# Splitting a table into three bf16 parts on ScalarE and TensorE in place of VectorE, in an embedding-bag kernel

## The chip, the cores and the metric

The kernel runs on one core of one Trainium2 chip. The metric is the device time of a whole execution in microseconds (us). The kernel before takes 1639.28 us (median of 3 runs, 1639.16 to 1640.66).

## The reference

There are 32 tables of 12,500 rows of 64 fp32 numbers, 512 bags for each table, and 20 row numbers and a length for each bag. The output is, for each bag and table, the sum of the rows that the first `length` numbers name.

```python
flat = tables.reshape(F_ * V_, E_)                    # F=32, V=12500, E=64
emb = flat[ids + offs]                                # ids: (B=512, F=32, L=20)
mask = (jnp.arange(L_) < lengths[..., None]).astype(emb.dtype)
pooled = jnp.einsum('bfle,bfl->bfe', emb, mask)
return jnp.nan_to_num(pooled.reshape(Bq, F_ * E_))
```

## The kernel before

The tables are divided between two methods that run side by side.

**Counted tables (M = 18).** A table is loaded whole, 128 partitions by J = 98 rows of E = 64, in seven chunks (`CHUNKS`) of 14 rows, 896 fp32 numbers in a partition. The bags are taken in two halves, h = 0 and 1. VectorE builds one-hot matrices from the row numbers (`onehots`, L625 and L627; `single`, L611 and L613), TensorE multiplies a pair of them (`count`, L444) into a bank pair in PSUM, and ScalarE copies these counts to SBUF as small numbers (`save_counts`, L422). Such a step is called a slot here: two one-hot matmuls, one copy on ScalarE, and eight or ten matmuls of the half before it. Those (`multiply`, L454) multiply the counts with the table, which stands in three bf16 parts so that fp32 is kept. A half has 21 slots in seven stages of three, with a short single eviction ahead; a table has 14 stages, 42 slots and 44 evictions, and 18 tables make 792 evictions. The counts of half h are multiplied while the counts of the next half are made.

The three parts are the upper 16 bits of each fp32 number, the rest after them, and what is left after the upper 16 bits of that rest. VectorE makes them with two subtractions for each chunk, `cut_rest` (L641) and `cut_low` (L649), at the stages that `CUTS` gives (3 to 12), some chunks in two pieces. VectorE works `AHEAD` = 2 stages ahead of TensorE, since there are two sets of one-hots. The counts go through `SETS` = 3 sets of bank pairs: TensorE's eviction n waits until eviction n - 3 has been saved.

**Gathered tables (14).** GpSimd (POOL) gathers rows by indirect DMA, up to 20 for each of 56 tiles of 128 bags (L379), into 8 buffers. VectorE adds a tile's rows (`add_rows`, L689) at fixed stages (`ADDS`, seven tiles for two counted tables); after each fourth tile GpSimd stores the results (`put`, L389). A buffer is refilled with zeros and row numbers by SyncE after its tile was added, and GpSimd takes the buffers in order. At the start GpSimd also writes 56 tiles of sorted records to DRAM (L365).

SyncE issues the loads of the tables: `reload` waits for TensorE to be done with the chunk of the table before. All waits are on semaphores, and each engine works in its own program order. TensorE's tables 1 to 17 are a loop (L495).

```python
free = n - (SETS - 2 if h == 0 and c == 0 and q < 1 else SETS - 1)
if not known(free, 1):
    pe.wait_ge(counts_saved, free)
```

Of the kernel before, what the change touches and what calls it, by code (L numbers as in the profile page):

```python
# [23 lines left out]
P = 128  # L24
# [3 lines left out]
SETS = 3  # L28
PARTS = 3
CHUNKS = 7  # L30
PER_CHUNK = 6
PAIRS = PER_CHUNK // 2
AHEAD = 2
# [7 lines left out]
CUTS = {3: (0, 0, 1), 4: (1, 0, 1), 5: (2, 0, 2), 6: (2, 1, 2), 7: (3, 0, 2), 8: (3, 1, 2), 9: (4, 0, 1),  # L41
        10: (5, 0, 2), 11: (5, 1, 2), 12: (6, 0, 1)}
# [33 lines left out]
def build_embedding_bag(nc, ids, lengths, tables, lookup_ids, lookup_lengths, lookup_place, ramps, triangle,  # L76
# [25 lines left out]
    assert STAGES % AHEAD == 0 and P_COLUMNS % 2 == 0 and L < 32 and LAST_BAGS == 4 and 2 * EVICTIONS % SETS == 2  # L102
# [17 lines left out]
    with ExitStack() as ctx:  # L120
# [21 lines left out]
        lane = sb("lane", [P, 1], I32)  # L142
        p_of = sb("p_of", [P, HALVES, P_COLUMNS], F16)
# [64 lines left out]
        rest_done = sem("rest_done")  # L208
        parts_ready = sem("parts_ready")
# [32 lines left out]
        def eviction_at(stage, q):  # L242

            return eviction(stage // STAGES, stage // CHUNKS % 2, stage % CHUNKS, q)

# [161 lines left out]
        def _(act):  # L407
# [15 lines left out]

            for f in range(M):
                for h in range(2):
                    save_counts(f, h, 0, -1)
                    for c in range(CHUNKS):
                        for q in range(PAIRS):
                            save_counts(f, h, c, q)

        @block.tensor
        def _(pe):
# [28 lines left out]

            def phase(f, h, with_counts=True, with_products=True):
# [29 lines left out]
            rank_lengths()  # L492
            phase(0, 0, with_products=False)
# [7 lines left out]
        def _(dve):  # L501
# [86 lines left out]

            def prepare(c):
# [40 lines left out]
            def upper_halves(t):  # L630
                return table[:, t, :].bitcast(BF16).rearrange("p (n x) -> p n x", x=2)[:, :, 1]

            cuts = [0]

            def cut_rest(f, c, part, parts):

                sl = slice(c * CE + part * CE // parts, c * CE + (part + 1) * CE // parts)
                if part == 0:

                    dve.wait_ge(table_in[c], f * 16 + 16)  # L640
# [4 lines left out]
            def cut_low(f, c, part, parts):  # L645
                sl = slice(c * CE + part * CE // parts, c * CE + (part + 1) * CE // parts)
# [142 lines left out]
```

## Time and profile before

| what | value |
|---|---|
| median of 3 runs | 1639.28 us |
| profiled execution: its own time, its span | 1622.87 us, 1621.1 us |
| mean granted TensorE clock | 0.792 |
| VectorE (DVE) busy | 1065.0 us, 66% |
| TensorE matmul (PE) busy | 1003.0 us, 62% |
| GpSimd (POOL) busy | 760.1 us, 47% |
| ScalarE (ACT) busy | 509.2 us, 31% |

The busy time of an engine is a sum over the whole span. PE's matmuls overlap, so that its busy time isn't a measure of its peak. The granted clock is 1.00 at 2.4 GHz and 0.50 at 1.2 GHz. "Releaser" is what ended the idle time of an engine; "remote" or "unknown queue" stands where the profile found no record that fits, and "issue" where the engine waited for nothing that the profile shows.

### The profile page before, as it was taken

What the parts mean: (1) busy time and instruction counts of PE and PEld (TensorE: products, weight loads), DVE (VectorE), ACT (ScalarE), POOL (GpSimd) and SP (SyncE); (2) the same over time, 40 slices, a digit from 0 to 9 for tenths busy, and PEclk for the clock granted to TensorE, in tenths of its full rate; (3) what the DMA queues carried; (4) which work ended last, traced back from release to release, by engine and by line L of the source; (5) the groups of instructions that cost most, each with busy time, mean ns of one, the idle gap of its engine ahead of it and who ended that gap; (6) DMA issues with size and microseconds to landing.
All of it is one profiled execution on the core that took longest, in us unless ns stands there. A gap on an engine that the chain in (4) does not pass through costs nothing.

```text
span 1621.1 us, 25785 instructions
## 1 busy us (share of the span) xinstructions
PE 1003.0 (62%) x8607; PEld 801.0 (49%) x8607; DVE 1065.0 (66%) x3021; ACT 509.2 (31%) x793; POOL 760.1 (47%) x706
## 2 busy tenths in 40 slices
PE   2757107692754816757588582881847538487886
PEld 0536006571643715636377360760735437276776
DVE  9938006793673916947599481891857629489894
ACT  2423004350422403324244140430423214143441
POOL 4845770537064172253666527166073442556110
PEclk9979558896786957968789685895877759689899
DMA  4312112132312213132334141231314113233120
GB/s 142 137 51 56 24 25 81 53 120 61 99 55 60 91 42 103 46 92 69 82 103 129 38 120 41 85 88 37 114 43 123 52 41 98 52 111 110 31 83 11
DMA packets 69225, 121.48 MB, mean 75 GB/s; under 512 B 33985, under 2 KB 35750, under 8 KB 69152
## 3 DMA queue, kind: packets, MB, share of 16 engines
q1 hardware_dynamic: 45936, 99.21, 19.0%
q0 software_dynamic: 22016, 20.93, 7.2%
q10 hardware_dynamic: 1200, 0.67, 0.2%
q14 instruction: 65, 0.53, 0.1%
q8 instruction: 8, 0.13, 0.0%
HBM read 79.67 MB, written 4.80 MB: 52 GB/s over the span
## 4 chain that ended last, share of the span: by engine, by line
DVE 44%; another core or an unknown queue 29%; PE 14%; issue 7%; DMA 2%; ACT 2%; SPq 1%; DVEq 0%; POOL 0%; POOLq 0%
DVE onehot_j L627 16%; PE sums L454 9%; DVE onehot_p L625 6%; DVE table L641 6%; DVE table L649 6%; DVE gathered L689 5%; PE pairs L444 4%; DMA table<-tables 2%; ACT counts L422 2%; DVE is_nan L659 1%; SPq L305 1%; DVE pooled L669 1%; DVE pooled L662 0%; DVEq L687 0%
## 5 line engine op out<-in xcount | busy, mean ns | idle before, releaser
L454 PE MATMUL sums<-table,counts 128*128 128x192 bf16 x7056 | 835.5, 262 | 209.3 <-issue 202.1
L422 ACT ACTIVATE counts<-pairs 128x588 int16<-128x588 f32 (+1 forms) x792 | 507.9, 653 | 1082.1 <-remote 547.1
L454 PEld LDWEIGHTS sums<-table,counts 128*128 128x128 fp8e3 x7056 | 667.0, 102 | 312.8 <-issue 258.3
L379 POOL DMA_INDIRECT rows<-tables,row_now x576 | 618.5, 1074 | 414.6 <-issue 414.6
L444 PE MATMUL pairs<-onehot_j,onehot_p 128*128 128x294 bf16 x1548 | 383.8, 315 | 390.2 <-ACT counts L422 164.4
L625 DVE TENSOR_TENSOR onehot_p<-ramp,p_of 128x256 bf16<-128x256 f16 x756 | 213.7, 283 | 435.1 <-remote 385.0
L627 DVE TENSOR_SCALAR onehot_j<-ramp,j_of,worth 128x296 bf16<-128x296 f16 x1512 | 493.6, 358 | 0.0
L444 PEld LDWEIGHTS pairs<-onehot_j,onehot_p 128*128 128x128 bf16 x1548 | 151.4, 101 | 488.5 <-issue 264.5
L389 POOL DMA_INDIRECT out_gathered<-gathered,place_now x56 | 70.2, 1254 | 394.0 <-DVE gathered L662 381.2
L641 DVE TENSOR_TENSOR table<-table 128x448 f32<-128x448 f32 (+1 forms) x180 | 144.4, 802 | 27.7 <-DMA table<-tables 27.0
L649 DVE TENSOR_TENSOR table<-table 128x448 f32<-128x448 f32 (+1 forms) x180 | 144.7, 804 | 0.0
L689 DVE TENSOR_REDUCE gathered<-rows 128x64 f32<-128x1280 f32 x56 | 131.2, 2343 | 0.0
L365 POOL DMA_INDIRECT sorted_records<-records,rank x56 | 69.3, 1238 | 33.7 <-DVE records L517 16.9
L669 DVE TENSOR_REDUCE pooled<-sums 128x128 f32<-128x384 f32 x36 | 19.7, 546 | 80.2 <-remote 67.4
L613 DVE TENSOR_SCALAR onehot_j<-ramp,j_of,worth 128x296 bf16<-128x296 f16 x36 | 13.1, 363 | 0.0
L611 DVE TENSOR_SCALAR onehot_p<-ramp,p_of 128x128 bf16<-128x128 f16 x36 | 11.0, 305 | 0.0
L662 DVE COPY_PREDICATED pooled<-is_nan,zeros 128x256 f32<-128x256 uint8 x18 | 8.1, 450 | 0.6
L659 DVE TENSOR_TENSOR is_nan<-pooled 128x256 uint8<-128x256 f32 x18 | 7.7, 427 | 0.6
L692 DVE COPY place_now<-row_now 128x1 int32<-128x1 int32 x56 | 8.1, 144 | 0.0
L662 DVE COPY_PREDICATED gathered<-is_nan,zeros 128x256 f32<-128x256 uint8 x14 | 6.2, 446 | 0.5
L659 DVE TENSOR_TENSOR is_nan<-gathered 128x256 uint8<-128x256 f32 x14 | 6.0, 426 | 0.5
L488 PE MATMUL sums<-counts 128*128 128x21 f16 x1 | 0.2, 177 | 8.2 <-DVE counts L536 8.2
(53 smaller groups left out, 49.0 us busy)
## 6 DMA issues: line engine op xcount, KB each, us to landing
table<-tables SPq DMA_DIRECT2D x126, 448.0 KB
rows<-zeros SPq DMA_DIRECT2D x56, 640.0 KB
rows<-tables,row_now POOLq DMA_INDIRECT x576
out_counted<-pooled SPq DMA_DIRECT2D x108, 21.0 KB
sorted_records<-records,rank POOLq DMA_INDIRECT x56
row_now<-sorted_records SPq DMA_DIRECT2D x56, 10.5 KB
out_gathered<-gathered,place_now POOLq DMA_INDIRECT x56
rows<-lookup_ids SPq DMA_DIRECT2D x1, 731.0 KB, 7.8
```

The lines of the kernel that those rows point to most:

```text
L365: nc.gpsimd.indirect_dma_start(out=sorted_records, out_offset=bass.IndirectOffsetOnAxis(ap=rank[:, t:t + 1], axis=0), in_=records[:, t, :] ...
L379: nc.gpsimd.indirect_dma_start(out=rows[:, k, l * E:(l + 1) * E], out_offset=None, in_=table_rows, in_offset=bass.IndirectOffsetOnAxis(ap= ...
L389: nc.gpsimd.indirect_dma_start(out=out_gathered, out_offset=bass.IndirectOffsetOnAxis(ap=place_now[:, k:k + 1], axis=0), in_=gathered[:, k ...
L422: nc.scalar.activation(dst, src, ACT.Copy).then_inc(counts_saved, 1)
L444: last = nc.tensor.matmul(pair(h, c, q)[:, x, 0:WIDE], onehot_p[:, s, k, :, side], onehot_j[:, s, i + 1, 0:WIDE], start=True, stop=True)
L454: last = nc.tensor.matmul(sums[h][:, k * PARTS * E:(k + 1) * PARTS * E], counts[h][:, j, :, k], parts[:, :, j, :, 1], start=(j == 0 and k ...
L625: nc.vector.tensor_tensor(onehot_p[:, s, 1 + i // 2, :, :], ramp_twice, p_of[:, 2 * f + h, g:g + 2].unsqueeze(1).to_broadcast([P, P, 2]), ...
L627: nc.vector.tensor_scalar(onehot_j[:, s, i + 1, :], ramp[:, 2 * P:], j_of[:, n:n + 1], worth[:, 0:1], ALU.is_equal, ALU.mult).then_inc(one ...
L641: nc.vector.tensor_tensor(table[:, 1, sl], table[:, 0, sl], upper_halves(0)[:, sl], ALU.subtract).then_inc(rest_done, 1)
L649: cut = nc.vector.tensor_tensor(table[:, 2, sl], table[:, 1, sl], upper_halves(1)[:, sl], ALU.subtract)
L669: nc.vector.tensor_reduce(out=pooled[:, 2 * h * E:2 * (h + 1) * E].rearrange("p (k e) -> p k e", e=E), in_=sums[h][:, 0:2 * PARTS * E].rea ...
L689: nc.vector.tensor_reduce(out=gathered[:, k * E:(k + 1) * E], in_=rows[:, k, :].rearrange("p (l e) -> p e l", e=E), axis=AX_X, op=ALU.add)
```

## The change

Six of the seven chunks of each table are parted by ScalarE and TensorE; VectorE keeps the seventh. ScalarE copies a chunk of fp32 numbers into a new bank pair in PSUM, `rest` (`copy_chunk`). TensorE subtracts the upper 16 bits there, with a matmul against a negative identity matrix that accumulates (`take_away`, two matmuls of 448 columns). ScalarE writes the upper 16 bits of the rest to the second part of the table (`save_middle`), TensorE takes that away, and ScalarE writes what is left to the third part (`save_low`). The chunk begun at slot u is copied at u, has its middle saved at u + 1 and its low part at u + 2; chunks begin at slots 9, 13, 17, 21, 25 and 29. On each engine these steps stand behind the slot's own work. VectorE parts chunk 6, whole, at stage 12. The new bank pair comes from the counts: `SETS` falls from 3 to 2. VectorE makes the negative identity once (`negate_eye`), and TensorE opens `rest` once (`begin_rest`).

```diff
-SETS = 3
+SETS = 2
-CUTS = {3: (0, 0, 1), 4: (1, 0, 1), 5: (2, 0, 2), 6: (2, 1, 2), 7: (3, 0, 2), 8: (3, 1, 2), 9: (4, 0, 1),
-        10: (5, 0, 2), 11: (5, 1, 2), 12: (6, 0, 1)}
+PARTED_AT = {0: 9, 1: 13, 2: 17, 3: 21, 4: 25, 5: 29}
+PARTED_BY_VECTOR = {12: 6}
...
+        minus_eye = sb("minus_eye", [P, P], BF16)
+        rest = psum("rest", [P, 2, 512], F32)
...
+            def copy_chunk(f, c):
+                if f == 0 and c == min(PARTED_AT):
+                    act.wait_ge(rest_begun, 1)
+                elif parted(f, c) > 1:
+                    act.wait_ge(low_saved, parted(f, c) - 1)
+                act.wait_ge(table_in[c], f * 16 + 16)
+                nc.scalar.activation(rest[:, :, 0:CE // 2], both_halves(0, c), ACT.Copy).then_inc(chunk_copied, 1)
+            def save_middle(f, c):
+                act.wait_ge(rest_ready, parted(f, c))
+                nc.scalar.activation(upper_of_both(1, c), rest[:, :, 0:CE // 2], ACT.Copy).then_inc(middle_ready, 1)
+            def save_low(f, c):
+                act.wait_ge(low_ready, parted(f, c))
+                nc.scalar.activation(upper_of_both(2, c), rest[:, :, 0:CE // 2], ACT.Copy).then_inc(low_saved, 1)
...
                             save_counts(f, h, c, q)
+                            u = slot(h, c, q)
+                            if u - 2 in begun_in:
+                                save_low(f, begun_in[u - 2])
+                            if u - 1 in begun_in:
+                                save_middle(f, begun_in[u - 1])
+                            if u in begun_in:
+                                copy_chunk(f, begun_in[u])
...
+            def take_away(part, c, done):
+                for x, half in enumerate(halves_of(c)):
+                    last = nc.tensor.matmul(rest[:, x, 0:CE // 2], minus_eye[:], upper_halves(part)[:, half],
+                                            start=False, stop=True, skip_group_check=True)
+                last.then_inc(done, 1)
+            def part_table(f, u):
+                if u - 2 in begun_in:
+                    pe.wait_ge(middle_ready, parted(f, begun_in[u - 2]))
+                    take_away(1, begun_in[u - 2], low_ready)
+                if u - 1 in begun_in:
+                    pe.wait_ge(chunk_copied, parted(f, begun_in[u - 1]))
+                    take_away(0, begun_in[u - 1], rest_ready)
...
-                                pe.wait_ge(parts_ready, f * CHUNKS + (c + 1))
+                                if c in PARTED_AT:
+                                    pe.wait_ge(low_saved, parted(f, c))
+                                else:
+                                    pe.wait_ge(parts_ready, f * (CHUNKS - PARTED) + by_vector.index(c) + 1)
                             multiply(1 - h, c * JC + q * JC // PAIRS, c * JC + (q + 1) * JC // PAIRS)
+                        if with_counts:
+                            part_table(f, slot(h, c, q))
...
-                    if stage in CUTS and i == 1:
-                        cut_rest(f, *CUTS[stage])
-                    if stage in CUTS and i == 4:
-                        cut_low(f, *CUTS[stage])
+                    if stage in PARTED_BY_VECTOR and i == 1:
+                        cut_rest(f, PARTED_BY_VECTOR[stage])
+                    if stage in PARTED_BY_VECTOR and i == 4:
+                        cut_low(f, PARTED_BY_VECTOR[stage])
```

## Rows read from the trace of the kernel before

**Rows 1.** The chain that ended last, by line, whole span.

```profile
by line: another core or an unknown queue 29.3%; DVE onehot_j L627 15.7%; PE sums L454 9.5%; issue 7.1%; DVE onehot_p L625 6.1%; DVE table L641 6.0%; DVE table L649 5.5%; DVE gathered L689 5.5%; PE pairs L444 4.2%; DMA table<-tables 2.1%; A
```

**Rows 2.** The waits: us in total, times, longest.

```profile
ACT counts L422 <- remote: 547.1, 66, 32.4
...
DVE onehot_p L625 <- remote: 385.0, 52, 32.1
```

**Rows 3.** Busy time of each engine in 27 stretches in which GpSimd gathers.

```profile
core 0: us, PE busy (x) PEld busy (x) DVE busy (x) ACT busy (x) POOL busy (x), PEclk, DMA share, GB/s
134.00:245.00 111.00, 28.75 (x182) 16.57 (x179) 24.31 (x75) 9.77 (x15) 85.72 (x83) 0.60 0.14 25
...
562.00:617.00 55.00, 12.19 (x90) 9.88 (x89) 13.41 (x40) 3.98 (x6) 42.58 (x41) 0.59 0.20 44
...
817.00:847.00 30.00, 24.46 (x250) 21.42 (x247) 29.70 (x84) 14.01 (x22) 24.21 (x20) 0.97 0.32 90
...
1598.00:1603.00 5.00, 5.00 (x61) 5.00 (x59) 0.00 (x0) 0.00 (x0) 3.79 (x4) 1.00 0.06 20
sum 876.00, PE 426.83 PEld 314.29 DVE 450.51 ACT 166.82 POOL 684.21; mean PE 15.81 PEld 11.64 DVE 16.69 ACT 6.18 POOL 25.34
```

**Rows 4.** The same for the 26 stretches between them.

```profile
245.00:291.00 46.00, 34.80 (x330) 30.80 (x331) 33.26 (x97) 20.61 (x32) 0.00 (x0) 0.83 0.28 85
...
1555.00:1598.00 43.00, 37.72 (x365) 31.73 (x363) 42.81 (x114) 18.84 (x29) 0.00 (x0) 0.96 0.13 36
sum 593.00, PE 493.69 PEld 425.62 DVE 506.22 ACT 294.87 POOL 4.47; mean PE 18.99 PEld 16.37 DVE 19.47 ACT 11.34 POOL 0.17
```

**Rows 5.** TensorE's timeline, first in a gathering stretch, then in one without.

```profile
192.29 0.32 PE L454 MATMUL sums<-table,counts 128*128 128x192 bf16 x1 [2.49 <-issue]
195.09 0.32 PE L454 MATMUL sums<-table,counts 128*128 128x192 bf16 x1 [2.47 <-issue]
...
264.00 0.41 PE L444 MATMUL pairs<-onehot_j,onehot_p 128*128 128x294 bf16 x2
264.24 1.02 PE L454 MATMUL sums<-table,counts 128*128 128x192 bf16 x10
...
267.14 0.41 PE L444 MATMUL pairs<-onehot_j,onehot_p 128*128 128x294 bf16 x2
```

**Rows 6.** Groups by line and shape: busy us, mean ns, idle before.

```profile
L422 ACT ACTIVATE counts<-pairs 128x588 int16<-128x588 f32 x756 | 496.4, 667 | 975.2 <-remote 475.9 <-PE pairs L444 444.8 <-issue 53.5
L627 DVE TENSOR_SCALAR onehot_j<-ramp,j_of,worth 128x296 bf16<-128x296 f16 x1512 | 493.6, 358 | 0.0
L625 DVE TENSOR_TENSOR onehot_p<-ramp,p_of 128x256 bf16<-128x256 f16 x756 | 213.7, 283 | 435.1 <-remote 385.0 <-issue 25.6 <-PE pairs L444 24.0
L689 DVE TENSOR_REDUCE gathered<-rows 128x64 f32<-128x1280 f32 x56 | 131.2, 2343 | 0.0
L649 DVE TENSOR_TENSOR table<-table 128x896 f32<-128x896 f32 x72 | 78.1, 1085 | 0.0
L641 DVE TENSOR_TENSOR table<-table 128x896 f32<-128x896 f32 x72 | 77.9, 1082 | 27.7 <-DMA table<-tables 27.0 <-issue 0.7
L649 DVE TENSOR_TENSOR table<-table 128x448 f32<-128x448 f32 x108 | 66.6, 617 | 0.0
L641 DVE TENSOR_TENSOR table<-table 128x448 f32<-128x448 f32 x108 | 66.6, 616 | 0.0
L422 ACT ACTIVATE counts<-pairs 128x196 int16<-128x196 f32 x36 | 12.3, 341 | 106.9 <-remote 71.2 <-PE pairs L444 35.2 <-issue 0.3
L379 POOL DMA_INDIRECT rows<-tables,row_now x576 | 618.5, 1074 | 414.6 <-issue 414.6
```

**Rows 7.** GpSimd's gathers and VectorE's work beside them, timeline.

```profile
353.29 2.34 POOL L379 DMA_INDIRECT rows<-tables,row_now  x1 [0.30 <-issue]
...
353.46 1.08 DVE L641 TENSOR_TENSOR table<-table 128x896 f32<-128x896 f32 x1
...
192.83 1.00 POOL L379 DMA_INDIRECT rows<-tables,row_now  x1 [0.30 <-issue]
```

More of the change, by code:

```diff
@@ L244, in eviction_at, with slot, parted, halves_of @@
             return eviction(stage // STAGES, stage // CHUNKS % 2, stage % CHUNKS, q)
+        def slot(h, c, q):
+            return (h * CHUNKS + c) * PAIRS + q
+        by_vector = sorted(PARTED_BY_VECTOR.values())
+        begun_in = {u: c for c, u in PARTED_AT.items()}
+        PARTED = len(PARTED_AT)
+        def parted(f, c):
+            return f * PARTED + sorted(PARTED_AT).index(c) + 1
+        def halves_of(c):
+            return [slice(c * CE + x * CE // 2, c * CE + (x + 1) * CE // 2) for x in range(2)]
+        def both_halves(part, c):
+            return table[:, part, c * CE:(c + 1) * CE].rearrange("p (x n) -> p x n", x=2)
+        def upper_halves(part):
+            return table[:, part, :].bitcast(BF16).rearrange("p (n x) -> p n x", x=2)[:, :, 1]
+        def upper_of_both(part, c):
+            return upper_halves(part)[:, c * CE:(c + 1) * CE].rearrange("p (x n) -> p x n", x=2)
         def lookup_group(c, i):
@@ L460, in multiply, with begin_rest @@
                     last.then_inc(table_used, 1)
+            def begin_rest():
+                pe.wait_ge(eye_ready, 1)
+                pe.wait_ge(ramps_in, 32)
+                for x in range(2):
+                    last = nc.tensor.matmul(rest[:, x, :], minus_eye[:], ramp[:, 0:512], start=True, stop=True)
+                last.then_inc(rest_begun, 1)
+            def take_away(part, c, done):
[10 more added lines that the diff above has]
+                    take_away(0, begun_in[u - 1], rest_ready)
             def phase(f, h, with_counts=True, with_products=True):
@@ L492, in _ @@
             rank_lengths()
+            begin_rest()
             phase(0, 0, with_products=False)
@@ L628, in onehots, with cut_rest @@
                                         ALU.is_equal, ALU.mult).then_inc(onehots_ready, 1)
-            def upper_halves(t):
-                return table[:, t, :].bitcast(BF16).rearrange("p (n x) -> p n x", x=2)[:, :, 1]
             cuts = [0]
[L635 to L640, printed above, removed]
+            def cut_rest(f, c):
+                sl = slice(c * CE, (c + 1) * CE)
+                dve.wait_ge(table_in[c], f * 16 + 16)
                 nc.vector.tensor_tensor(table[:, 1, sl], table[:, 0, sl], upper_halves(0)[:, sl],
@@ L643, in cut_rest, with cut_low @@
                 cuts[0] += 1
-            def cut_low(f, c, part, parts):
-                sl = slice(c * CE + part * CE // parts, c * CE + (part + 1) * CE // parts)
+            def cut_low(f, c):
+                sl = slice(c * CE, (c + 1) * CE)
                 dve.wait_ge(rest_done, cuts[0])
-                cut = nc.vector.tensor_tensor(table[:, 2, sl], table[:, 1, sl], upper_halves(1)[:, sl], ALU.subtract)
-                if part == parts - 1:
-                    cut.then_inc(parts_ready, 1)
+                nc.vector.tensor_tensor(table[:, 2, sl], table[:, 1, sl], upper_halves(1)[:, sl],
+                                        ALU.subtract).then_inc(parts_ready, 1)
             cleaned = [0]
```

15 lines of the change are left out of this document (13 added, 2 removed).

## Prediction

> **What bounds the kernel now.** The chain that ended last is read first. Its largest part has no name: 29.3% stands under an unknown queue, and VectorE's cuts are only 6.0% and 5.5% [rows 1]. The waits say where that part lies: VectorE's L625 sat 385.0 us and ScalarE's L422 547.1 us until something for which the profile has no record [rows 2]. Both wait for TensorE's pair matmuls, so I cut the span by what GpSimd does.
>
> In 27 stretches, 876 us in all, GpSimd gathers; in the 26 between them, 593 us, it doesn't [rows 3, 4]. (134 us lie ahead and 18 behind.) ScalarE's count of instructions is the progress: one for each of the 792 evictions. By their starts 253 fall into the gathering stretches, 467 between them, and 72 ahead. So an eviction takes 876/253 = 3.46 us beside gathers and 593/467 = 1.27 us without. The stretch 562 to 617 is the extreme, 6 evictions in 55 us; 817 to 847 is the mild one, 22 in 30 [rows 3]. TensorE's own rows show the same: in the slow part one matmul of 192 columns each 2.8 us, with "issue" ahead of it, where otherwise ten take 0.86 us [rows 5]. What exactly holds TensorE beside the gathers I can't read; that it comes with them, I can. GpSimd's work is fixed, so these 876 us stay nearly whatever the others do. The kernel isn't bound by VectorE over its span, though VectorE's 66% is the highest: that is a mean over two regimes.
>
> Without gathers three slots of TensorE take 3.14 us (264.00 to 267.14) [rows 5]: 44 evictions make 44 x 1.053 = 46.3 us a table (the single one is shorter, which I leave out). VectorE's slot is 283 + 2 x 358 = 1.00 us by durations; by starts, less, since they overlap. VectorE's cuts are 78.1 + 77.9 + 66.6 + 66.6 = 289.2 us, 16.1 a table [rows 6]. VectorE and TensorE are thus near to each other, with VectorE somewhat longer in stages with cuts.
>
> **The change, part by part.**
>
> *VectorE's cuts.* Six of seven chunks go: 6/7 x 289.2 = 248 us of busy time. What of it is on the path? Between gathers the mean granted clock, weighted over the rows, is 0.858: 28% of 593, or 168 us, at half rate (1.2 GHz) [rows 4]. There TensorE needs 2.11 us an eviction and does 80. The other 425 us hold 387, 1.10 each, against TensorE's own 1.053. So VectorE can cost at most 0.045 x 387 = 17 us there. In the first half of table 0 nothing is multiplied and VectorE sets the pace: three chunks' cuts stand there (stages 3 to 6), 6 x 1.08 us by durations; I take 6 us off.
>
> *TensorE's new matmuls.* Four of 448 columns for each of six chunks, 24 a table. The pair matmuls of 294 columns follow each other such that two take 0.24 us at full clock (264.00 to 264.24) [rows 5], 0.122 each, so 448 columns take 0.187 by their columns: 4.5 us a table, 0.102 us an eviction. The 467 evictions between gathers then cost: 168 us at half rate do 168/2.31 = 73, and 394 at 1.155 take 455. That is 623 us, 30 more than 593, with VectorE's 17 us already given back. The bounds are +13 (half-rate time shrinks to half) and +48 (the 0.045 stays as hand-over time).
>
> *ScalarE.* 18 operations of 896 elements a table. From 667 ns at 588 elements and 341 at 196 [rows 6] the slope is 0.832 ns and the start 178 ns: 923 ns, 16.6 us a table, 299 in all, beside 509. In the four slots of a chunk ScalarE has 4 x 0.667 + 3 x 0.923 = 5.44 us, TensorE 4 x 1.053 + 0.75 = 4.96. Durations overlap, so I take this at 0; if they did not, 108 x 0.48 = 52 us come on top. Each save waits for TensorE behind its slot, with the next save of counts behind it on ScalarE; TensorE needs that one only two slots later. This cover is gone where a hand-over takes over one slot.
>
> *Two bank sets.* TensorE may be one slot ahead of ScalarE's saves, not two. Without gathers nothing is lost by it; beside them, where ScalarE saw a count late by several us, it is.
>
> *GpSimd.* A gather has 1074 ns in the mean and 1.00 us when alone; the one that met the cut L641 took 2.34 [rows 7]. If all were 1.00, 576 x 0.074 = 43 us would go. Most of the causes go (L625 stays): I take -25, bounds 0 and -43. The Trainium skill (SBUF — State Buffer, Who interferes with whom) says that a VectorE instruction with two SBUF inputs contends with a GpSimd instruction that reads SBUF; these rows agree.
>
> *Progress beside gathers.* In seven of the 27 stretches VectorE was at least 97% busy (529, 645, 817, 1239, 1351, 1447 and 1547): 57 evictions in 87 us. The other twenty hold 196 in 789 us, 4.0 us each. After the change VectorE is never the slowest: 1.00 us a slot against TensorE's 1.155 and ScalarE's load. I take the 87 us to go as the others: 22 evictions, 35 fewer. Each is made up between gathers at 623/467 = 1.33 us: +47 us. Bounds: all at the pace of 562 to 617 (9.2 us each) leaves 95 of 253, +210; from below, the half of today's slowing gone, 876/(3.46/2) = 506, -337. The near rows are the other twenty, so I stay by +47. The reader should doubt this term most: that an idle VectorE goes with a slow TensorE is seen, which causes which isn't.
>
> *Table loads.* VectorE's 27.0 us of waits for them [rows 6] go; they fell behind slow stretches, where TensorE had work. The copy of chunk 0 is at slot 9, after its load is in. 0 us.
>
> **The sum**, on the profiled span: 1621 + 30 - 6 - 25 + 47 = 1667 us. The median is 18 us above this span (1639.28 against 1621.1, in this one execution), so 1685 us.
>
> **The rivals.**
>
> *The stretches with gathers keep their progress.* For it: their length is GpSimd's, and TensorE is slow in them also when VectorE is full (1239 to 1250). Without the +47: 1620, or 1638 in the median, no change by what this kernel's measurement can tell (0.2%, 3 us), with 20 us on both sides.
>
> *Faster: the cuts are on the path after all.* The chain counts L641 and L649 with 11.5% of the span [rows 1]; 6/7 of it is 160 us, so 1461, or 1479 in the median. It decides if VectorE's lead, not TensorE, is what the slow stretches eat: VectorE works on in their first us and would later be the one that is behind. Against it: the sum above allows 17 us between gathers. The Trainium skill (the same page and section) says that TensorE never waits on anyone's port; by it the slow stretches would be no contention and only VectorE's 248 us would count, 1391 us in the median. The matmul each 2.8 us speaks against it.
>
> *Faster: fewer, longer matmuls load TensorE's path less beside gathers.* 14 matmuls in 1.43 us of such a slot against 12 in 1.05. If a third of 253 evictions more got through, 84 x 1.33 = 112 us go from 1620: 1508, 1526; for half of that 1564 and 1582. Nothing in the profile shows the onset well enough to refuse it.
>
> *Slower by hand-overs.* Beside gathers, a chunk crosses from TensorE to ScalarE and back twice. 253/792 of 108 chunks are 34; if each crossing costs TensorE an eviction's 3.46 us once, 34 x 2 x 3.46 = 235 us are lost there, and a third of it not covered is 78 us: 1745 us, or 1763. With ScalarE's 52 us 1815. It decides when a hand-over exceeds one slot.
>
> **How the numbers follow.** Forecast 0.42 (1650 to 1725); hand-overs 0.14 (1725 to 1815); unchanged stretches 0.18 (1615 to 1650; a third each faster, same, slower); more getting through 0.15 (1520 to 1615); cuts on the path 0.11 (1390 to 1520). Faster: 0.06 + 0.15 + 0.11 = 0.32, and 0.03 from the low edge of the forecast's bounds, 0.35. Same 0.06. Slower the rest, 0.59. The forecast's own range is 1650 to 1725. The range reaches down to 1550 and up to 1765: it leaves out 0.15 below and some 0.05 above.
>
> **What would show it.** VectorE's busy time near 817 us and ScalarE's near 808; TensorE with 432 matmuls more; a slot between gathers of 1.15 us a row at full clock; gathers at a mean of 1.03; and, decisive, ScalarE's instructions that save counts in the stretches with gathers: some 218 where there were 253. The forecast is wrong if these rise, or if the slots between gathers take less than 1.1 us, or if the stretches with gathers themselves become shorter than some 850 us.

## The result, and the profile after

The kernel after takes 1820.01 us (median of 4 runs, 1817.8 to 1823.82), the kernel before 1639.22 beside it: a ratio of 1.113, 95% interval 1.106 to 1.120. The forecast was 1685 (1550 to 1765). It is slower, as was thought likeliest, but by four times as much as forecast. Where the executions of a kernel scatter by more than 1.5%, the ratios are of its faster executions alone, and so can differ a little from the ratio of two medians.

One thing has to be said at once, though it was found last: the comparisons fell on several chips. In five of seven (the first, and chips 10, 14, 0 and 8) the kernel before has a median of 1613 to 1639 us; in the other two, on chips 6 and 9, it takes 1095. The kernel after was run on one of these two, chip 9, and takes 1026 there, a ratio of 0.937. What follows explains the first, and then the second.

The page of the kernel after, busy time of each engine, TensorE's clock by fortieths, and the chain by engine:

```profile
PE 1051.3 (58%) x9041; PEld 852.6 (47%) x9041; DVE 870.6 (48%) x2698; ACT 809.6 (45%) x1117; POOL 700.3 (39%) x706
...
PEclk9778559787777958779677786767967769678899
...
another core or an unknown queue 35%; PE 35%; ACT 13%; DVE 10%; issue 6%; POOL 0%; DVEq 0%; POOLq 0%
```

No engine is over 58% busy, and a large part of the chain still has no name (29.3% before [rows 1], 35% now). Its waits, which answer to [rows 2]:

```profile
DVE onehot_p L715 <- remote: 588.9, 74, 32.8
ACT counts L455 <- remote: 506.1, 63, 33.0
POOL out_gathered L422 <- DVE gathered L746: 427.5, 14, 58.1
...
PE pairs L500 <- ACT counts L455: 247.6, 61, 26.4
...
PE rest L528 <- ACT table L467: 170.5, 90, 25.5
```

VectorE's wait without a record has grown by 204 us; that is more than the whole loss. The busy time by stretches answers to [rows 3] and [rows 4]: first those in which GpSimd gathers, then those between.

```profile
core 0: us, PE busy (x) PEld busy (x) DVE busy (x) ACT busy (x) POOL busy (x), PEclk, DMA share, GB/s
156.00:262.00 106.00, 15.30 (x95) 10.24 (x92) 6.51 (x22) 8.64 (x11) 81.32 (x82) 0.54 0.13 26
...
sum 815.00, PE 278.09 PEld 215.55 DVE 195.94 ACT 152.49 POOL 626.78; mean PE 7.95 PEld 6.16 DVE 5.60 ACT 4.36 POOL 17.91
```

```profile
267.00:324.00 57.00, 46.71 (x440) 39.77 (x440) 38.20 (x127) 39.30 (x55) 0.40 (x2) 0.88 0.23 69
...
sum 824.00, PE 681.54 PEld 570.09 DVE 581.52 ACT 584.00 POOL 9.99; mean PE 20.05 PEld 16.77 DVE 17.10 ACT 17.18 POOL 0.29
```

Beside gathers TensorE is busy 278 of 815 us where it was 427 of 876 [rows 3], and VectorE, 451 of 876 before, is now busy 196. The stretches with gathers are shorter, but less gets done in them. The evictions are counted as the prediction did, by the starts of ScalarE's saves of counts. The stretches are taken here by the exact starts and ends of the gathers, so that before has 252 in 873 us where the text ahead has 253 in 876; a stretch ends where GpSimd pauses for over 1.5 us.

| | ahead | beside gathers | between | behind | end |
|---|---|---|---|---|---|
| before | 134 us | 873 us, 252 (3.46 each) | 596 us, 468 (1.27) | 18 | 1621 |
| after | 156 us | 819 us, 148 (5.53) | 820 us, 574 (1.43) | 21 | 1816 |

The 195 us are thus: 106 more evictions between gathers, 106 x 1.27 = +135; the stretches with gathers, -54; the pace between gathers, (1.43 - 1.27) x 574 = +89; +22 ahead and +3 behind. (Each kernel is measured here by one profiled execution, as above.)

The groups by line and shape, which answer to [rows 6]:

```profile
L412 POOL DMA_INDIRECT rows<-tables,row_now x576 | 578.1, 1004 | 619.8 <-issue 619.5 <-DMA row_now<-sorted_records 0.3
L455 ACT ACTIVATE counts<-pairs 128x588 int16<-128x588 f32 x756 | 492.3, 664 | 694.3 <-remote 488.0 <-PE pairs L500 180.1 <-issue 24.9
...
L471 ACT ACTIVATE table<-rest 128x896 bf16<-128x896 f32 x108 | 127.8, 1183 | 122.8 <-remote 102.8 <-PE rest L528 14.0 <-issue 0.5
L467 ACT ACTIVATE table<-rest 128x896 bf16<-128x896 f32 x108 | 127.1, 1177 | 122.0 <-remote 90.0 <-PE rest L528 15.2 <-issue 10.3
L463 ACT ACTIVATE rest<-table 128x896 f32<-128x896 f32 x108 | 100.4, 929 | 0.0
```

ScalarE's copy into PSUM takes 929 ns, as the slope in the prediction said (923), but its two saves to the table take 1183 and 1177. And a gather takes 1.00 us in the mean. TensorE's timeline in a stretch without gathers, at full clock, shows what a chunk costs (611.93 to 617.48 are four slots):

```profile
611.93 0.41 PE L500 MATMUL pairs<-onehot_j,onehot_p 128*128 128x294 bf16 x2
...
612.13 1.18 ACT L467 ACTIVATE table<-rest 128x896 bf16<-128x896 f32 x1
...
613.37 0.57 PE L528 MATMUL rest<-table,minus_eye 128*128 128x448 bf16 x2 [0.17 <-ACT table L467]
...
613.77 0.41 PE L500 MATMUL pairs<-onehot_j,onehot_p 128*128 128x294 bf16 x2
...
613.97 1.19 ACT L471 ACTIVATE table<-rest 128x896 bf16<-128x896 f32 x1
...
616.08 0.95 ACT L463 ACTIVATE rest<-table 128x896 f32<-128x896 f32 x1
...
617.48 0.41 PE L500 MATMUL pairs<-onehot_j,onehot_p 128*128 128x294 bf16 x2
```

Four slots with a chunk take 5.55 us, where the prediction had 4.96 for TensorE alone. The two new matmuls take 0.40 us (613.37 to 613.77), 0.80 for both hand-overs; the other 0.5 us are TensorE's waits for ScalarE. Its L467 starts at 612.13 and ends at 613.31, behind TensorE's ten matmuls, and its copy L463 ends at 617.03, behind the next ten. A save of 1.18 us doesn't fit under one slot of some 1.05.

### The profile page after: what moved, and what is told of

The parts are those of the page before. It is cut to its first block, busy times and chain, and to the rows that moved or that the text cites. A ratio compares the mean times of both kernels' runs of the same rounds, so it can differ in the third digit from the quotient of the medians.

```text
span 1816.0 us, 26781 instructions
## 1 busy us (share of the span) xinstructions
PE 1051.3 (58%) x9041; PEld 852.6 (47%) x9041; DVE 870.6 (48%) x2698; ACT 809.6 (45%) x1117; POOL 700.3 (39%) x706
## 4 chain that ended last, share of the span: by engine, by line
another core or an unknown queue 35%; PE 35%; ACT 13%; DVE 10%; issue 6%; POOL 0%; DVEq 0%; POOLq 0%
PE sums L510 21%; PE pairs L500 8%; ACT table L467 6%; PE rest L528 6%; ACT counts L455 4%; DVE onehot_j L717 4%; ACT table L471 2%; DVE gathered L773 2%; DVE onehot_p L715 2%; ACT rest L463 1%; DVE table L734 1%; DVE table L726 0%; DVE onehot_j L703 0%; DVE onehot_p L701 0%
## 5 line engine op out<-in xcount | busy, mean ns | idle before, releaser
L412 POOL DMA_INDIRECT rows<-tables,row_now x576 | 578.1, 1004 | 619.8 <-issue 619.5
L510 PE MATMUL sums<-table,counts 128*128 128x192 bf16 x7056 | 800.8, 262 | 23.5 <-issue 23.5
L500 PE MATMUL pairs<-onehot_j,onehot_p 128*128 128x294 bf16 x1548 | 358.5, 315 | 413.3 <-ACT counts L455 247.6
L717 DVE TENSOR_SCALAR onehot_j<-ramp,j_of,worth 128x296 bf16<-128x296 f16 x1512 | 472.3, 354 | 0.0
L528 PE MATMUL rest<-table,minus_eye 128*128 128x448 bf16 x432 | 136.0, 399 | 309.3 <-ACT table L467 170.5
L422 POOL DMA_INDIRECT out_gathered<-gathered,place_now x56 | 59.0, 1054 | 440.4 <-DVE gathered L746 427.5
L528 PEld LDWEIGHTS rest<-table,minus_eye 128*128 128x128 bf16 x432 | 29.0, 101 | 353.3 <-ACT table L467 195.5
L471 ACT ACTIVATE table<-rest 128x896 bf16<-128x896 f32 x108 | 127.8, 1183 | 122.8 <-remote 102.8
L467 ACT ACTIVATE table<-rest 128x896 bf16<-128x896 f32 x108 | 127.1, 1177 | 122.0 <-remote 90.0
L463 ACT ACTIVATE rest<-table 128x896 f32<-128x896 f32 x108 | 100.4, 929 | 0.0
L734 DVE TENSOR_TENSOR table<-table 128x896 f32<-128x896 f32 x18 | 19.6, 1087 | 0.0
L726 DVE TENSOR_TENSOR table<-table 128x896 f32<-128x896 f32 x18 | 19.6, 1087 | 0.0
L703 DVE TENSOR_SCALAR onehot_j<-ramp,j_of,worth 128x296 bf16<-128x296 f16 x36 | 12.7, 352 | 0.0
```

The source lines that it names most:

```text
L412: nc.gpsimd.indirect_dma_start(out=rows[:, k, l * E:(l + 1) * E], out_offset=None, in_=table_rows, in_offset=bass.IndirectOffsetOnAxis(ap= ...
L463: nc.scalar.activation(rest[:, :, 0:CE // 2], both_halves(0, c), ACT.Copy).then_inc(chunk_copied, 1)
L467: nc.scalar.activation(upper_of_both(1, c), rest[:, :, 0:CE // 2], ACT.Copy).then_inc(middle_ready, 1)
L471: nc.scalar.activation(upper_of_both(2, c), rest[:, :, 0:CE // 2], ACT.Copy).then_inc(low_saved, 1)
L500: last = nc.tensor.matmul(pair(h, c, q)[:, x, 0:WIDE], onehot_p[:, s, k, :, side], onehot_j[:, s, i + 1, 0:WIDE], start=True, stop=True)
L510: last = nc.tensor.matmul(sums[h][:, k * PARTS * E:(k + 1) * PARTS * E], counts[h][:, j, :, k], parts[:, :, j, :, 1], start=(j == 0 and k ...
```

## The experiments

The theory made after the result, called A, is this: what slows TensorE is GpSimd gathering at its full rate, one gather each 1.30 us; VectorE's two-input subtractions held gathers up, and TensorE got through meanwhile. Taking them away let GpSimd gather undisturbed. Its rivals are the hand-overs, ScalarE's longer work and the lost set of banks.

Each kernel below ran on the chip named, together with the kernel before. The last column counts matmuls started for each us between the starts of two indirect DMAs of GpSimd (gathers and stores of results), in gaps of 1.25 to 1.33 us and in gaps of 1.4 to 3 us. "Saves" are the saves of counts beside gathers, of 792, with the length of those stretches.

| run | chip | us | ratio, interval | saves beside gathers | mean gather, us | matmuls a us, gaps of 1.3 / over 1.4 (number of these) |
|---|---|---|---|---|---|---|
| before | first | 1639 | | 252 in 873 us | 1.07 | 2.6 / 7.5 (124) |
| after | first | 1820 | 1.113, 1.106 to 1.120 | 148 in 819 | 1.00 | 2.3 / 7.7 (12) |
| two_sets | 10 | 1629 | 1.009, 1.003 to 1.015 | 256 in 871 | 1.07 | 2.3 / 7.2 (121) |
| cuts_once | 10 | 1608 | 1.005, 1.000 to 1.009 | 150 in 824 | 1.01 | 2.5 / 6.5 (35) |
| cover | 10 | 1679 | 1.046, 1.034 to 1.058 | 261 in 873 | 1.07 | 2.4 / 7.7 (115) |
| cover_one | 14 | 1762 | 1.085, 1.080 to 1.090 | 178 in 834 | 1.02 | 2.2 / 7.4 (53) |
| after_rest | 0 | 1592 | 0.980, 0.973 to 0.988 | 655 in 1270 | 1.06 | 0.6 / 6.2 (525) |
| before_rest | 0 | 1634 | 1.005, 1.002 to 1.009 | 663 in 1330 | 1.17 | 0.5 / 5.5 (512) |
| after_again | 9 | 1026 | 0.937, 0.936 to 0.939 | 694 in 854 | 1.05 | 9.4 / 9.3 (116) |

(In the two with _rest, gaps of 1.3 us are left only between GpSimd's stores, some 40 of them.)

**The parts of the change by themselves.** *two_sets* is the kernel before with two bank sets:

```diff
-SETS = 3
+SETS = 2
```

> The kernel before with SETS = 2 in place of 3 and nothing else. If the loss of the third bank pair is what makes TensorE slow beside the gathers, this shows a good part of the 11%: some 1720 us or more, and fewer than 253 evictions in the gathering stretches. If the loss comes from an idle VectorE or from the hand-overs, it stays within 1% of before (1625 to 1655).

Measured: 1.009. The lost set costs some 15 us (5 to 25 by the interval), and leaves the evictions beside gathers as they were (256).

*cuts_once* is the kernel before with six chunks parted in table 0 alone. Tables 1 to 17 use table 0's middle and low parts, so their sums lack their own lower bits; the work of TensorE is the same, and it waits for a chunk's load where it waited for its parts. The edit of the first cut (the second has the same condition):

```diff
-                    if stage in CUTS and i == 1:
+                    if stage in CUTS and i == 1 and (f == 0 or CUTS[stage][0] == CHUNKS - 1):
...
```

> The kernel before, in which six of the seven chunks are parted in table 0 only; the later tables are multiplied with the middle and low parts of table 0, and TensorE waits for the load in place of the cuts. VectorE has the load of the kernel after, and TensorE and ScalarE have nothing new. If an idle VectorE makes the gathers hold TensorE more, it is slower than before: 1650 to 1700 us, with some 220 evictions or fewer beside gathers. If only TensorE's and ScalarE's new work counts, it is faster than before by up to 1 to 3% (1590 to 1625), with 253 or more.

Measured: 1.005, no change, though VectorE is rid of 199 us (866.4 busy for 1065.0). Neither expectation fits whole: the evictions beside gathers fell as the first said (150 for 252), and the time stayed as the second said. Between gathers an eviction takes 1.12 us where it took 1.27, at nearly the same granted clock there (0.85 and 0.86): VectorE's cuts did cost something there. Gain and loss cancel. This kernel has none of the new matmuls, hand-overs or ScalarE work, so the fewer evictions beside gathers come from taking VectorE's work away.

**Giving VectorE useless work.** *cover* is the kernel after with subtractions of zeros where the cuts stood:

```diff
+IDLE_CUTS = {3: 1, 4: 1, 5: 2, 6: 2, 7: 2, 8: 2, 9: 1, 10: 2, 11: 2}
...
+                    if stage in IDLE_CUTS and i in (1, 4):
+                        n = CE // IDLE_CUTS[stage]
+                        dve.wait_ge(unused_written, idle[0])
+                        idle[0] += 1
+                        nc.vector.tensor_tensor(unused[:, 0:n], zeros[:, 0:n], upper_of_zeros[:, 0:n],
+                                                ALU.subtract).then_inc(unused_written, 1)
```

> The kernel after, to which VectorE's cuts are added back as work of no use: the same subtractions of two SBUF inputs at the same stages, on zeros, into a tile that nobody reads. If VectorE's two-input work is what kept TensorE going beside gathers, the kernel gets faster than after although it does more, by 20 to 100 us of the 181. If VectorE's idleness is only a sign, it stays at 1820 or gets slower by up to 20 us.

Measured: 1.046; in a second comparison (*cover_again*) 1.036, 1.029 to 1.043. Work that nobody needs takes the kernel after from 1.113 to 1.046 and 1.036 of the kernel before, 109 to 125 us (20 to 100 were expected). Its rows:

```profile
L415 POOL DMA_INDIRECT rows<-tables,row_now x576 | 618.5, 1074 | 471.2 <-issue 471.2
...
L798 DVE TENSOR_TENSOR unused<-zeros 128x896 f32<-128x896 f32 (+1 forms) x324 | 254.0, 784 | 0.0
...
sum 874.00, PE 403.15 PEld 319.37 DVE 407.56 ACT 285.74 POOL 682.80; mean PE 13.90 PEld 11.01 DVE 14.05 ACT 9.85 POOL 23.54
```

Gathers are back at 1074 ns and TensorE's busy time beside them at 403 us (427 before, 278 after), with 261 evictions. The new matmuls, ScalarE's work and two bank sets are all still there: beside a busy VectorE they are worth what is left, some 4 to 5%.

Four kernels, put side by side, show that the loss needs both halves of the change (ratios to the kernel before):

| | VectorE does the work of the cuts | VectorE is rid of it |
|---|---|---|
| without the new work of TensorE and ScalarE | 1 (before) | 1.005 (cuts_once) |
| with it, and two bank sets | 1.046 and 1.036 (cover) | 1.113 (after) |

Freeing VectorE costs nothing by itself, the new work 4 to 5%, both together 11%. Beside gathers the new work changes nothing once VectorE is free (150 evictions in cuts_once, 148 in after). It tells between gathers, where an eviction takes 1.12 us in cuts_once and 1.43 in after: 0.31 x 574 = 178 us, nearly the whole difference of the two spans (1613 and 1816 us), with 22 us ahead as the rest. Freeing VectorE pushes some 100 evictions out from beside the gathers; the new work takes away the faster pace that would have paid for them.

*cover_one* has the same with one input (`tensor_scalar(unused, upper_of_zeros, 1.0, None, ALU.mult)`).

> The kernel after, with useless work on VectorE in the old places and of about the old length, but each operation reads one input (a multiplication of zeros by one) where the run before had two-input subtractions. Theory A (it is VectorE's two-input operations that hold GpSimd's gathers up, and TensorE gets through in that time): nothing is held up, gathers stay at a mean near 1.00 us, some 150 of the 792 saves of counts lie beside gathers, ratio to the kernel before 1.10 to 1.13. Rival B (any work of VectorE there, or its later one-hots, keeps TensorE going): as with the two-input cover, some 260 beside gathers, ratio 1.03 to 1.06.

Measured: 1.085, between the two. It doesn't part theory from rival, since these operations took three fifths of the time of the others (465 ns for 784):

```profile
L415 POOL DMA_INDIRECT rows<-tables,row_now x576 | 586.8, 1019 | 556.3 <-issue 556.3
...
L798 DVE TENSOR_SCALAR unused<-zeros 128x896 f32<-128x896 bf16 (+1 forms) x324 | 150.7, 465 | 0.0
```

But it stands in nearly one order with the others: in after, cuts_once, cover_one, cover and before the gaps of 1.4 us or more number 12, 35, 53, 115 and 124, and the saves beside gathers 148, 150, 178, 261 and 252.

**Without the gathers.** *before_shallow* and *after_shallow* cut all depths to 1: 56 gathers in place of 576, and the gathered tables' sums lack the other rows.

```diff
-                step(nc.vector.tensor_scalar(depth_f, depth_f, 1.0, None, ALU.max))
+                step(nc.vector.tensor_scalar(depth_f, depth_f, 1.0, 1.0, ALU.max, ALU.min))
```

> The kernel after with one gather for each tile in place of up to 20 (56 in place of 576; the gathered sums are of one row). If slow TensorE comes from the gathers, nearly all of the 815 us of gathering stretches beyond their 143 evictions go: 792 x 1.3 to 1.4, some 1050 to 1150 us. If something in the new hand-overs holds TensorE without gathers, it stays above 1300.

> The kernel before with every depth cut to 1, so that GpSimd gathers once for a tile and not up to 20 times (56 gathers of 576); the sums of the gathered tables leave out all rows but the first. It stands against the kernel after with the same cut, 0.707 of the kernel before. Theory A (without gathers the change costs little: both are bound by TensorE or VectorE at some 1.2 us a slot): ratio 0.68 to 0.72. Rival (the hand-overs between TensorE and ScalarE and the lost bank set cost TensorE 70 us wherever it runs): ratio 0.64 to 0.67. Third (the change is a gain without gathers, since VectorE is what binds there): ratio 0.73 to 0.78.

Measured: 1137 us, 0.707 (0.700 to 0.714), and 1117, 0.689 (0.686 to 0.692). So 520 gathers cost the kernel before some 500 us and the kernel after 680. Without them the change costs about 20 us by the medians and some 30 by the ratios (the two ran on different chips, 10 and 14). The pages, the kernel after first, each with its chain by engine:

```profile
PE 961.4 (85%) x9041; PEld 801.2 (70%) x9041; DVE 861.3 (76%) x2698; ACT 806.0 (71%) x1117; POOL 179.7 (16%) x186
...
PE 59%; ACT 16%; DVE 15%; another core or an unknown queue 7%; issue 2%; POOL 0%; DVEq 0%; POOLq 0%
```

```profile
PE 923.5 (83%) x8607; PEld 764.7 (69%) x8607; DVE 1050.2 (94%) x3021; ACT 514.5 (46%) x793; POOL 213.8 (19%) x186
...
DVE 81%; another core or an unknown queue 7%; PE 4%; DMA 2%; issue 2%; SPq 1%; DVEq 1%; POOL 0%; POOLq 0%
```

VectorE, 94% busy and 81% of the chain, is what holds the kernel before there; the kernel after has relieved it and is held by TensorE and its hand-overs to ScalarE (59% and 16% of the chain).

**The rate of the gathers.** Theory A says that any slower rate would do. *after_paced* and *before_paced* put a register load behind every second gather:

```diff
+                        if l % 2:
+                            pool.value_load(depth[0:1, bass.ds(b + column(k), 1)], min_val=1, max_val=L)
```

> The kernel after, with one useless register load on GpSimd behind every second gather, which puts about 0.3 us between two gathers; VectorE's work is unchanged. Theory A (the rate of the gathers is what stops TensorE, and VectorE matters only by slowing them): more than 200 saves of counts beside gathers where the kernel after has some 145, and a time below its own: ratio to the kernel before 1.03 to 1.09. Rival B (TensorE is slow beside gathers at whatever rate, by something that VectorE's work itself relieves): the stretches with gathers become longer by 240 x 0.3 = 72 us and bring no more saves each, ratio 1.11 to 1.16.

> The kernel before with the same register load behind every second gather. Theory A: its stretches with gathers become longer, but it gets more through than 253; where GpSimd has time to spare (it waits for gathered rows), the time falls, ratio 0.95 to 0.99. Rival B: longer stretches with no more in them, ratio 1.00 to 1.05.

Measured: 1.113 (1.109 to 1.117) and 0.987 (0.982 to 0.993). Neither tests the theory: the load is hidden, gathers still start 1.30 us apart, and the kernel after has its 148 saves beside gathers again. The kernel after does repeat its first ratio on another chip. Why the kernel before came out 1.3% lower isn't explained; its trace has the same parts (257 in 872 us, 463 in 584).

*after_rest* and *before_rest* have real work on GpSimd, and a wait for its end, behind every gather. *before_drain* has `pool.drain()` there.

```diff
+                        nc.gpsimd.iota(unused[:], pattern=[[1, 140]], base=0, channel_multiplier=0).then_inc(rested, 1)
+                        pool.wait_ge(rested, 1)
+                        pool.sem_clear(rested)
```

> The kernel after, with an iota of 140 elements on GpSimd behind every gather and a wait for its end, since the register load of an earlier run left gathers 1.30 us apart. In the traces so far TensorE starts some 2.4 matmuls in a us between two gathers 1.30 us apart (after 1591 in 705 us) and 7 to 8 where VectorE's work has held the gather up to 1.4 us or more (before 1603 in 216 us). Theory A (gathers at full rate outrun something that TensorE also needs, and any slower rate leaves it nearly whole): with some 1.8 to 2.0 us from gather to gather over 6 matmuls a us beside them, the stretches with gathers become 576 x 0.6 = 345 us longer and hold over 500 of the 792 saves; ratio to the kernel before 0.88 to 1.00. Rival B (each gather takes a fixed time of some 0.9 us from TensorE, at whatever rate): the stretches become longer, TensorE gets its own pace in the added time alone, and the ratio stays 1.08 to 1.14. Rival C (only VectorE's work relieves TensorE): as many matmuls a us as in the kernel after, ratio over 1.15.

> The kernel before with the same iota and wait behind every gather. Theory A: over 6 matmuls a us beside gathers, ratio 0.83 to 0.95. Rival B: ratio 0.97 to 1.03. Rival C: ratio over 1.05.

> The kernel before with a drain of GpSimd's own pipeline behind every gather and no iota: a smaller step, perhaps 0.1 to 0.3 us from gather to gather on top of 1.30. Theory A: between the kernel before and the run with the iota, ratio 0.90 to 0.99. Rival B: 0.98 to 1.02.

GpSimd's timeline in after_rest:

```profile
641.23 1.05 POOL L414 DMA_INDIRECT rows<-tables,row_now  x1 [0.86 <-POOL unused L418]
642.29 0.27 POOL L418 IOTA unused<- 128x140 int32 x1
643.42 1.02 POOL L414 DMA_INDIRECT rows<-tables,row_now  x1 [0.86 <-POOL unused L418]
```

Measured: after_rest 1591.9 us, 0.980. Slowing GpSimd to 2.19 us from gather to gather (641.23 to 643.42) takes the kernel after from 1.113 to 0.980 of the kernel before, 216 us. VectorE's work is the same as there, so it is the gathers' rate that stops TensorE, and VectorE matters by setting it. TensorE starts 6.2 matmuls a us where it started 2.3 beside gathers. Even that is a mean of two kinds of gaps: of 487 gaps of 2.0 to 2.5 us between gathers, 127 have no matmul, and 309 have 14 to 27. Rival B's fixed price of some 0.9 us for each gather would leave TensorE about 1.3 of the 2.2 us, some 13 matmuls at 10 a us, so it is refused. What holds after_rest now is GpSimd, shown by VectorE's wait for gathered rows and TensorE's for VectorE's one-hots:

```profile
ACT counts L460 <- PE pairs L505: 479.2, 288, 42.9
DVE gathered L778 <- DMA out_gathered<-gathered,place_now: 448.6, 12, 44.4
POOL rows L414 <- POOL unused L418: 423.2, 490, 0.9
...
PE pairs L505 <- DVE onehot_j L722: 343.4, 25, 42.0
```

That is also why before_rest gains nothing (1.005): TensorE goes at 5.5 a us, but GpSimd's rows come late, and with VectorE's subtractions back a gather takes 1168 ns where after_rest has 1064, 576 x 0.104 = 60 us more. With equal pauses the change is thus a gain, 42 us. The expected 0.83 to 0.95 for it was wrong: GpSimd's 2.2 us a gather is itself 1250 us and more. before_drain took 2323 us (1.431): with the drain GpSimd is idle for 2.4 us ahead of each gather where it was for 0.3, so it adds 2.1 us and not 0.1 to 0.3, and GpSimd bounds that kernel.

**The two chips on which TensorE isn't stopped.** *after_rest2*, *before_rest2* (iota behind every second gather, `if l % 2`) and *after_rest3* (every third) were to find the best pause:

> The kernel after with the iota and its wait behind every second gather. With it behind each, gathers came 2.17 us apart, GpSimd bound the kernel (VectorE waited 586 us for gathered rows) and TensorE started 6.2 matmuls a us. Theory A (two gathers 1.30 us apart and then a pause still leave TensorE most of its pace): GpSimd's part falls to 576 x 1.74 = 1000 us, TensorE's own 1137 us (the run with one gather a tile) is near the bound, ratio to the kernel before 0.78 to 0.93. Rival B (what counts is each gather at full rate; half of them stop TensorE as before): ratio 0.98 to 1.06.

> The kernel before with the iota and its wait behind every second gather. Theory A: ratio 0.80 to 0.95. If the change costs TensorE nothing once gathers are paced, it is not faster than the kernel after with the same pause; if the hand-overs and the bank set cost what they did beside the useless cover (3 to 5 per cent), it is 40 to 70 us faster than that.

> The kernel after with the iota and its wait behind every third gather only (1.59 us from gather to gather in the mean). Theory A in a smooth form: between the kernel after (1.11) and the run with every second, 0.88 to 1.00. Theory A with an onset (TensorE keeps its pace through the first four gathers of a burst and loses it behind them, so that a pause within every four is enough): as fast as with every second or faster, since GpSimd has less to do, 0.76 to 0.88.

Measured: 1268, 1325 and 1177 us. But the kernel before took 1094.5 us beside them (7 runs, 1093.1 to 1095.7), not some 1620: ratios of 1.158, 1.211 and 1.076. None of the expected ratios is met. Here every pause only costs, the more of them the more; with equal pauses the kernel after is again the faster, by 57 us. So the next comparison was with the kernel after itself:

> The kernel after, unchanged, beside the kernel before once more, since in the last comparison the kernel before took 1094 us and not some 1620. Where the kernel before takes 1620 us, ratio 1.10 to 1.125 again. Where it takes 1094: if all of the loss was the gathers stopping TensorE (theory A), VectorE, which is then nearly full in the kernel before, is relieved and the ratio is 0.97 to 1.01; if the hand-overs, ScalarE's longer operations and the lost bank set cost what the runs with one gather a tile say (1137 us after against 1117 before), 1.01 to 1.04.

> The kernel after with the iota and its wait behind every third gather, once more, to have it beside the kernel after on one chip. Where the kernel before takes 1620 us: theory A in a smooth form 0.97 to 1.05 (between the kernel after and the pause behind every gather, 0.98), with an onset behind the fourth gather 0.80 to 0.95. Where the kernel before takes 1094: 1.07 to 1.08 again, and slower than the kernel after, since there the pauses only lengthen GpSimd's part.

It fell on another chip where the same holds: before 1095.7 us, after_rest3b 1179.0 (1.076, 1.074 to 1.078), as expected for this case, and the kernel after 1026.5 us, 0.937, a larger gain than theory A (0.97 to 1.01) or its rival (1.01 to 1.04) had. Its page and rows of waits:

```profile
PE 935.2 (91%) x9041; PEld 784.8 (77%) x9041; DVE 867.3 (85%) x2698; ACT 805.4 (79%) x1117; POOL 725.8 (71%) x706
...
PEclk9999999999999999999999999999999999999998
...
PE 68%; ACT 15%; DVE 14%; issue 2%; POOL 0%; DVEq 0%; POOLq 0%
```

```profile
POOL rows L412 <- issue: 188.3, 576, 13.1
ACT counts L455 <- PE pairs L500: 154.8, 330, 7.5
DVE onehot_p L715 <- PE pairs L500: 116.4, 212, 1.0
...
PE rest L528 <- ACT table L467: 24.6, 104, 0.8
```

It is the same program. Now GpSimd gathers almost in one stretch, 854 us, with 694 evictions at 1.23 us each, TensorE starts 9.4 matmuls a us between gathers 1.3 us apart, the waits without a record are gone, and the granted clock is full in all slices but the last, where it sank to 0.5 and 0.6 in slices in which TensorE was stopped. TensorE, 91% busy and 68% of the chain, bounds it. The kernel before has VectorE's 1065 us of work in a time of 1095, so VectorE most likely bounds it; that is not shown, since no trace of it on such a chip was taken (*before_again* was meant to be one).

> The kernel before, unchanged, for its trace in the condition of the last comparisons. If it takes 1095 us again: VectorE, with some 1065 us of work, is busy over 95% of the span and TensorE waits for its one-hots; GpSimd works through without long waits. If it takes 1620 again, the trace repeats the one of before.

> The kernel after with the useless two-input subtractions on VectorE. Where the kernel before takes 1095 us: VectorE's 1070 us bind it again, 1090 to 1120 us, ratio 1.00 to 1.02, some 70 us slower than the kernel after, so that the same work costs time here and saved 141 us where TensorE was stopped. If another cause than VectorE's time decided the gain of 6% (the bank sets, the clock), the ratio stays near 0.94. Where the kernel before takes 1620: 1.03 to 1.06 again.

Measured: 1.000 (0.997 to 1.004) and 1.036, on chip 8, where it is stopped again; they repeat the first results. So whether useless work costs time where TensorE isn't stopped wasn't seen.

**A version that beats both.** Where TensorE is stopped, after_rest does, by 2% (0.980). Where it isn't, the kernel after itself is the fastest (0.937), and a pause behind every third gather costs it 15%. What after_rest3 would do where TensorE is stopped wasn't tried.

## Why the prediction was wrong

- *Progress beside gathers* is the step that failed: "22 evictions, 35 fewer", +47 us. Measured: 104 fewer (148 for 252), moved between gathers at 1.27 to 1.33 us, 132 to 138 us. The argument took only the seven stretches where VectorE was full to be changed. But the cuts worked in the others too, by holding up gathers: of the 124 gaps of over 1.4 us in the kernel before, 96, with 1186 of their 1603 matmuls, lie in the other twenty. The row of 2.34 us beside a cut [rows 7] was read as GpSimd's loss alone, -25 us, when it was TensorE's chance. Both terms are one mechanism with the other sign. The text said to doubt this term most, for the right reason.
- *GpSimd*: the mean gather came out at 1.00 us (expected 1.03), and the gathering stretches shortened by 54 us (expected 25). The two terms together were forecast at +22 and came to about +81.
- *VectorE's cuts*, "at most 17 us" between gathers, failed: cuts_once shows 1.12 us for 1.27, 73 us on 468 evictions. The 17 came from charging all half-rate time at twice TensorE's 1.053 us. The same reckoning of cuts_once (569 evictions in 636 us at a clock of 0.85) leaves 0.92 us for an eviction at full clock, less than TensorE's own 1.053, so half-rate time was charged too high. The change could have earned this back; the next point took it.
- *ScalarE at 0 on the path* failed: two saves take 1.18 us each, not 0.92, and four slots with a chunk take 5.55 us, not 4.96. That is 0.59 us a chunk, 64 us in 108 at full clock; the bound of +52 was nearer than the value. With *TensorE's new matmuls* (+30) and *two bank sets* (0; some 15 us by two_sets) the pace between gathers became 1.43 where 1.33 was reckoned, +89 for +30.
- *Ahead*, where the forecast had -6 us, +22 came up that no term had; GpSimd's scatters lie there. Where TensorE isn't stopped, gathers begin at 112 us in after_again and at 113 in before_rest2, so these 22 us seem to hang on the stop too; they aren't taken apart further.
- The rival that came nearest by number, hand-overs (1763 to 1815), put the loss beside gathers, and there it isn't: cuts_once has no hand-overs and 150 evictions there, the kernel after 148. They cost between gathers. The rival "the cuts are on the path" is what holds on chip 9, with 69 us, not 160, since TensorE is next at once.
- VectorE's busy time is 870.6, not 817: the 248 us were a sum of durations, and some of them overlapped with one-hots. ScalarE's (809.6 for 808) is right by luck: its durations add up to 870.6 us, since the saves are longer, and 61 us of them overlap.

The Trainium skill (SBUF — State Buffer, Who interferes with whom) says that TensorE never waits on anyone and that DMA doesn't contend with a compute engine. The prediction set a row against it. In the traces of four comparisons the kernels without pauses bear the row out (2.2 to 2.8 matmuls a us between gathers 1.3 us apart), and that of after_again bears out the page (9.4). That the ports are what differs is not shown.

**What stays open** is what stops TensorE. One thing differs with it: the trace of after holds 10,604 records of semaphore updates, that of the same program where TensorE isn't stopped 20,448, and after_rest, half relieved, 16,620. Of the 9,844 fewer in after, 9,495 are landings of DMA transfers (6,390 for 15,885); both hold 26,781 records of instructions. So where gathers stop TensorE, records are also being lost. The Trainium skill (NOTIFIC — the notification-queue block, Overflow: three behaviours, one of which stalls the engine) says that the block through which engines report events holds its producers back when its inner queues fill, rather than lose a record there. By that it could be the recording of a gather's many events that stops TensorE, and the rate would matter as it does here; the loss of records would then need another reason. No run was made without a recording, so this is argued, not shown. Nor is it shown whether the chip decides or something else that changed with it: the two comparisons without the stop (chips 6 and 9) followed each other within seven minutes, after those on the first chip, 10, 14 and 0 and ahead of that on chip 8, so it could as well have been the time.

## What to carry over

An idle engine's work can be what paces another: before freeing an engine beside a shared bottleneck, ask what its work delays, and test with useless work in its place (one run, and the answer has a sign). Read the kernel's own progress in each regime, and forecast each with its own price; a gain in one regime (1.12 us for 1.27 in cuts_once) can be eaten in the other. And if a stop has no name in the profile, find out whether it is there everywhere: the same change was +11% on one chip and -6% on another.

## Hardware behaviour that was not expected

- Beside indirect gathers 1.30 us apart, TensorE keeps its pace through the first four of a burst (8.5 matmuls a us in the kernel after) and then falls to 1.9 and below; in the kernel before, with held gathers among them, it goes at 9.1, 6.5, 5.0 and 2.8 by fours. In after_again it stays at 9.1 to 10.8 throughout.
- The kernel before had medians of 1613 to 1639 us in five comparisons and 1095 in two, on other chips.
- An fp32 subtraction on VectorE with two SBUF inputs, on data that nobody reads, raised GpSimd's mean gather from 1.00 to 1.07 us (cover); with one input and three fifths of the time, to 1.02 (cover_one).
- ScalarE wrote 896 bf16 numbers from PSUM to every second 16-bit place of SBUF in 1.18 us, and 896 fp32 numbers from SBUF to PSUM in 0.93.
- A register load between GpSimd's gathers cost nothing; a drain added 2.1 us, and an iota of 0.27 us with a wait for it 0.89.
